# An eight-part network on one core: two VectorE programs written out without a loop, and the depthwise convolutions as 64x64 quarters

## What is computed

```python
x = x + window_attention(layernorm(x))          # layer 0: 7x7 windows, 4 heads
t = t + top2_of_8_experts(layernorm(t))         # 128x128 matrix for each expert
x = x + focal_modulation(layernorm(x))          # layer 1, below
t = t + recurrence(layernorm(t))                # 3136 steps in time, 32 in parallel

# focal modulation
y = x @ Wf + bf; q, ctx, gates = split(y)
for l, k in enumerate((k0, k1, k2)):            # depthwise 3x3, 5x5, 7x7
    ctx = gelu(depthwise_conv(ctx, k))
    ctx_all += ctx * gates[l]
ctx_all += gelu(mean_over_pixels(ctx)) * gates[3]
out = layernorm(q * (ctx_all @ Wh + bh)) * gamma + beta
out = out @ Wp + bp
```

## Time and profile before

| | |
|---|---|
| median of 3 runs | 8981.09 us (8978.25 to 9027.3) |
| the profiled execution | 8979.28 us, span 8977.5 us |
| granted TensorE clock, mean | 0.973 |
| busy | PE 90%, DVE 70%, POOL 64%, PEld 54%, ACT 50% |
| experts, about | 1.81 to 3.87 ms of the span |
| convolutions, about | 4.45 to 6.04 ms |
| focal output, about | 6.06 to 7.10 ms |

### The profile page before, as it was taken

The page is one execution under the profiler, slowest core; times in us unless marked ns, Lnnn a source line. Parts: engine busy times, 40 slices in busy tenths (PEclk is TensorE's granted clock), DMA queues, the critical chain, the costliest instruction groups (busy, mean ns, idle before and its releaser), DMA issues. The chain is left out here.

```text
span 8977.5 us, 330977 instructions
## 1 busy us (share of the span) xinstructions
PE 8051.4 (90%) x112719; PEld 4838.4 (54%) x112719; DVE 6262.3 (70%) x21127; ACT 4513.2 (50%) x12517; POOL 5701.4 (64%) x6959
## 2 busy tenths in 40 slices
PE   7999999978889898779799999988888788888888
PEld 6777777744444444357544444436666555555554
DVE  8999999979999999878656666656777622222222
ACT  5666666645555555469733333335555433333333
POOL 8999999968888888778622222225666644444444
PEclk9999999989999999989999999999999899999999
DMA  1222222211111111258844554538777422222221
GB/s 52 57 57 57 58 58 58 59 53 54 54 54 54 51 53 54 69 183 301 286 163 164 180 181 164 180 124 214 200 203 200 121 55 55 56 56 56 56 55 53
DMA packets 797656, 955.86 MB, mean 106 GB/s; under 512 B 323100, under 2 KB 661825, under 8 KB 773584
## 3 DMA queue, kind: packets, MB, share of 16 engines
q1 hardware_dynamic: 797264, 952.06, 34.7%
HBM read 574.81 MB, written 453.35 MB: 115 GB/s over the span
## 5 line engine op out<-in xcount | busy, mean ns | idle before, releaser
L982 PE MATMUL moe_pe_out<-moe_we,moe_xnT 128*128 128x512 f32 x3136 | 1530.2, 621 | 232.3 <-DVE moe_acc L876 224.9
L1587 PE MATMUL conv_pc<-conv_c,conv_toep 64*64 64x416 f32 (+1 forms) x6896 | 1335.6, 534 | 4.2 <-ACT conv_c L1488 2.7
L778 ACT ACTIVATE moe_scaled<-moe_pe_out,moe_gate 128x128 f32<-128x128 f32 x3136 | 892.5, 368 | 792.8 <-PE moe_pe_out L982 791.1
L2287 ACT ACTIVATE rec_yT<-rec_ph 128x32 f32<-128x32 f32 x3136 | 618.4, 197 | 1251.5 <-PE rec_ph L2408 1251.5
L1443 POOL TENSOR_TENSOR conv_g<-conv_c,conv_gate 128x896 f32<-128x896 f32 x128 | 365.3, 2854 | 1212.2 <-DVE conv_out L1557 1174.6
L982 PEld LDWEIGHTS moe_pe_out<-moe_we,moe_xnT 128*128 128x128 f32 x3136 | 558.5, 195 | 1032.1 <-issue 1023.8
L298 POOL TENSOR_SCALAR att_xn<-att_xin,att_mv,att_rstd 128x128 f32<-128x128 f32 x1024 | 1007.1, 997 | 54.2 <-POOL att_rstd L294 54.2
L2408 PE MATMUL rec_ph<-rec_yT,rec_vt 128*32 128x32 f32 x25080 | 853.1, 207 | 196.6 <-ACT rec_yT L2287 121.8
L2334 DVE COPY rec_xT<-rec_pin 128x512 f32<-128x512 f32 x196 | 135.6, 692 | 1250.5 <-PE rec_pin L2380 1250.5
L2408 PEld LDWEIGHTS rec_ph<-rec_yT,rec_vt 128*32 128x32 f32 x25080 | 506.5, 108 | 647.5 <-ACT rec_yT L2287 609.9
L1587 PEld LDWEIGHTS conv_pc<-conv_c,conv_toep 64*64 64x64 f32 (+1 forms) x6896 | 487.9, 144 | 604.8 <-issue 535.2
(11 more groups left out here) (210 smaller groups left out, 19573.4 us busy)
## 6 DMA issues: line engine op xcount, KB each, us to landing
conv_toep<-rows_dram SPq DMA_DIRECT2D x32, 2304.0 KB, 13.9
c<-foc_cs SPq DMA_DIRECT2D x32, 1792.0 KB, 10.9
conv_cin<-c SPq DMA_DIRECT2D x32, 1792.0 KB, 8.9
ctx_all<-conv_out SPq DMA_DIRECT2D x32, 1792.0 KB, 7.0
att_xin<-x_windows SPq DMA_DIRECT2D x512, 98.0 KB
moe_xin<-x SPq DMA_DIRECT2D x112, 448.0 KB, 3.5
x<-moe_acc SPq DMA_DIRECT2D x112, 448.0 KB, 2.7
foc_xin<-x SPq DMA_DIRECT2D x32, 1568.0 KB, 8.3
```

The lines of the kernel that those rows point to most:

```text
L778: ins = act.activation(scaled[:, b, e, :], pe_out[:, b, 1, e * C:(e + 1) * C], ACT.Identity, scale=g)
L982: pe.matmul(pe_out[:, b, half, :], xnT[:, n.slot(2), t, :], we[:, half * 4:half * 4 + 4, :].rearrange("d e c -> d (e c)"), start=True, sto ...
L1587: return pe.matmul(image_pairs(pc[k], half)[m0:m1, :, i0:i1], w, tile[r0:r1, images(half), i0 + away:i1 + away], start=start, stop=(rows ! ...
L2287: act.activation(yT[:, a, cs], ph[:, a, cs], ACT.Sigmoid).then_inc(moved, 1)
```

## The change

In the experts' and the focal output's stage VectorE's steps are written out one after the other, with constant waits, by a new helper `straight_steps`. The other engines keep their loops. In the convolutions each product is now of 64 input and 64 output partitions, 60 in a channel, and the average is four such products (`average_low`, `average_high`). The filters' halves are interleaved in a new order; three semaphores (`firsts_made`, `thirds_made`, `half_averaged`) keep the two row halves of one bank apart in time. ScalarE takes `gelu2` ahead of the average and of `gelu3_plain`.

```diff
@@ -80,6 +80,15 @@
         for u in range(unroll):
             step(Step(it, unroll, u), MANY, -MANY)
     for n in range(rounds * unroll, count):
+        step(Step(0, unroll, n), n, n - count)
+
+
+def straight_steps(count, unroll, step):
+
+
+
+
+    for n in range(count):
         step(Step(0, unroll, n), n, n - count)
 
 
@@ -947,7 +956,7 @@
                 if last < -3:
                     layer_stats_end(n + 3)
 
-            run_steps(dve, N, U, step, 4)
+            straight_steps(N, U, step)
 
         @block.tensor
         def _(pe):
@@ -1370,7 +1379,7 @@
         rows_made = S.sems("rows_made", 2)
         group_in, toep_in, c0_in = S.sems("group_in", 2), S.sems("toep_in", 2), S.sems("c0_in", 2)
         convolved = S.sems("convolved", 3)
-        corners_made = S.sem("corners_made")
+        firsts_made, thirds_made, half_averaged = S.sem("firsts_made"), S.sem("thirds_made"), S.sem("half_averaged")
         activated = S.sems("activated", 3)
         gated1, gated2, gated3 = S.sem("gated1"), S.sem("gated2"), S.sem("gated3")
         pooled_part, averaged, glob_ready = S.sem("pooled_part"), S.sem("averaged"), S.sem("glob_ready")
@@ -1503,13 +1512,12 @@
                     gelu2(n, 0)
                 if last < -3:
                     gelu1(n + 2, first + 2)
+                if last < -2:
+                    gelu2(n + 1, first + 1)
                 if first >= 1:
                     average(n - 1, first - 1)
                 if last < -1:
                     gelu3_plain(n, first)
-                if last < -2:
-                    gelu2(n + 1, first + 1)
-                if last < -1:
                     gelu3_swapped(n)
 
             run_steps(act, N + 1, U, step, AHEAD)
@@ -1585,7 +1593,7 @@
                 if k == 2 and half == 1:
                     m0, m1 = ROW - m0, ROW - m0 + ROW
                 return pe.matmul(image_pairs(pc[k], half)[m0:m1, :, i0:i1], w,
-                                 tile[r0:r1, images(half), i0 + away:i1 + away], start=start, stop=(rows != ALL), skip_group_check=True)
+                                 tile[r0:r1, images(half), i0 + away:i1 + away], start=start, stop=True, skip_group_check=True)
 
             def ready(k, n, first):
                 g = Step(n.loop, U // PER, n.off // PER)
@@ -1596,40 +1604,13 @@
                 if k > 0:
                     hold(pe, activated[k - 1], n.val(1, 1), ticks)
                 if first >= 1:
-                    pe.wait_ge(activated[k], n.val())
-
-            def centre(k, n, first):
+                    hold(pe, activated[k], n.val(), ticks)
+
+            def whole(k, n, first):
+
                 ready(k, n, first)
                 for half in range(2):
                     block_of(k, n, half, 0, start=True)
-
-            def middle_plain(n, first):
-                ready(2, n, first)
-                for away in (0, 1, -1):
-                    block_of(2, n, 0, away, start=(away == 0))
-
-            def middle_swapped(n):
-
-                for away in (0, 1, -1):
-                    for outs in (LOW, HIGH):
-                        block_of(2, n, 1, away, outs=outs, start=(away == 0))
-
-
-            def four(crossed, straight):
-
-
-
-
-                (k, n, half, far), (j, m, part, low, high) = crossed, straight
-                block_of(k, n, half, -far, HIGH, LOW)
-                block_of(j, m, part, low, LOW, HIGH if j == 2 else LOW)
-                second = block_of(j, m, part, high, HIGH, LOW if j == 2 else HIGH)
-                first = block_of(k, n, half, far, LOW, HIGH)
-                return first, second
-
-            def whole(k, n, first):
-
-                centre(k, n, first)
                 for half in range(2):
                     if k == 0:
                         block_of(0, n, half, -1, HIGH, LOW)
@@ -1639,12 +1620,68 @@
                             ins = block_of(1, n, half, away)
                 ins.then_inc(convolved[k], 1)
 
-            def average(n, first):
-                if first >= 1:
-                    pe.wait_ge(glob_ready, n.val())
-                    pe.sem_inc(ticks, 1)
-                pe.wait_ge(pooled_part, n.val(1, 1))
-                pe.matmul(pm[:, 0:B], ones[:], pooled[:], start=True, stop=True).then_inc(averaged, 1)
+            def first_filter(n, low, high, start):
+
+
+
+                block_of(0, n, high, 0, HIGH, LOW, start)
+                block_of(0, n, low, 0, LOW, LOW, start)
+                block_of(0, n, high, 0, HIGH, HIGH, start)
+                block_of(0, n, low, 0, LOW, HIGH, start)
+                block_of(0, n, high, -1, HIGH, LOW)
+                return block_of(0, n, low, 1, LOW, HIGH)
+
+            def second_filter(n, low, high, start):
+
+
+
+                block_of(1, n, low, 0, LOW, LOW, start)
+                block_of(1, n, high, 0, HIGH, HIGH, start)
+                block_of(1, n, high, 0, HIGH, LOW, start)
+                block_of(1, n, low, -1, LOW, LOW)
+                block_of(1, n, high, -1, HIGH, HIGH)
+                block_of(1, n, low, 0, LOW, HIGH, start)
+                block_of(1, n, high, -1, HIGH, LOW)
+                block_of(1, n, low, 1, LOW, LOW)
+                block_of(1, n, high, 1, HIGH, HIGH)
+                return block_of(1, n, low, 1, LOW, HIGH)
+
+            def third_filter_on_own_rows(n):
+
+
+
+                for away in (0, -1, 1):
+                    block_of(2, n, 1, away, HIGH, HIGH, away == 0)
+                    block_of(2, n, 0, away, LOW, LOW, away == 0)
+                    block_of(2, n, 1, away, HIGH, LOW, away == 0)
+                    block_of(2, n, 0, away, LOW, HIGH, away == 0)
+                block_of(2, n, 1, -2, HIGH, LOW)
+                block_of(2, n, 0, 2, LOW, HIGH).then_inc(thirds_made, 1)
+
+            def third_filter_on_other_rows(n):
+
+                block_of(2, n, 0, -2, HIGH, LOW)
+                block_of(2, n, 1, 2, LOW, HIGH)
+                for away in (0, -1, 1):
+                    block_of(2, n, 0, away, HIGH, LOW)
+                    block_of(2, n, 1, away, LOW, HIGH)
+                    block_of(2, n, 0, away, HIGH, HIGH)
+                    ins = block_of(2, n, 1, away, LOW, LOW)
+                ins.then_inc(convolved[2], 1)
+
+            def average_low(n, first):
+                if first >= 1:
+                    hold(pe, glob_ready, n.val(), ticks)
+                hold(pe, pooled_part, n.val(1, 1), ticks)
+                for m0 in (0, ROW):
+                    ins = pe.matmul(pm[m0:m0 + ROW, 0:B], ones[0:ROW, 0:ROW], pooled[0:ROW, :], start=True, stop=False)
+                ins.then_inc(half_averaged, 1)
+
+            def average_high(n):
+                hold(pe, half_averaged, n.val(1, 1), ticks)
+                for m0 in (0, ROW):
+                    ins = pe.matmul(pm[m0:m0 + ROW, 0:B], ones[ROW:P, 0:ROW], pooled[ROW:P, :], start=False, stop=True)
+                ins.then_inc(averaged, 1)
 
             def step(n, first, last):
                 has1, has2, has3 = last < -3, last < -2, last < -1
@@ -1653,37 +1690,27 @@
                     whole(0, n + 1, 1)
                     whole(1, n, 0)
                 if has1:
-                    centre(0, n + 2, first + 2)
+                    ready(0, n + 2, first + 2)
+                    first_filter(n + 2, 0, 1, True)
                 if has2:
-                    centre(1, n + 1, first + 1)
+                    ready(1, n + 1, first + 1)
+                    second_filter(n + 1, 0, 1, True).then_inc(firsts_made, 1)
+                if has3:
+                    ready(2, n, first)
+                    third_filter_on_own_rows(n)
+                if first >= 1:
+                    average_low(n - 1, first - 1)
+                if has2:
+                    hold(pe, firsts_made, n.val(1, 1), ticks)
                 if has1:
-                    four((0, n + 2, 0, 1), (1, n + 1, 0, -1, 1))
-                    made1, made2 = four((0, n + 2, 1, 1), (1, n + 1, 1, -1, 1))
-                    made1.then_inc(convolved[0], 1)
-                    made2.then_inc(corners_made, 1)
-                elif has2:
-                    for half in range(2):
-                        block_of(1, n + 1, half, -1, LOW, LOW)
-                        made2 = block_of(1, n + 1, half, 1, HIGH, HIGH)
-                    made2.then_inc(corners_made, 1)
+                    first_filter(n + 2, 1, 0, False).then_inc(convolved[0], 1)
+                if has2:
+                    second_filter(n + 1, 1, 0, False).then_inc(convolved[1], 1)
+                if first >= 1:
+                    average_high(n - 1)
                 if has3:
-                    middle_plain(n, first)
-                if first >= 1:
-                    average(n - 1, first - 1)
-                if has3:
-                    middle_swapped(n)
-                if has2:
-                    hold(pe, corners_made, n.val(2, 1), ticks)
-                    made2, _ = four((1, n + 1, 0, 1), (1, n + 1, 1, 1, -1))
```

(13 more changed lines are left out.)

## The result

The changed kernel takes 8689.54 us (median of 4 runs, 8688.08 to 8727.33), the kernel before 8979.67 beside it: a ratio of 0.9676 with a 95% interval of 0.9634 to 0.9718, 290 us less. The forecast was 8748 and the low end of its range 8695, so the direction and the mechanisms held and the gain was larger than the range allowed.

The account below looks back on a forecast made before the run. VectorE (93% busy) was full in the experts, TensorE (100%) in the convolutions, no engine in the focal output, where something interrupts all. 8979.3 - 80 - 100 - 84 + 33 = 8748 us; range 8695 to 8870.

Parts of the forecast that it names:

- Experts without a loop: Experts' stage: removing VectorE's 24 loop returns and the slower steps behind them saves 80 us.
- With 16.65 us for a written-out step: Experts' stage: 96 steps go from 17.48 to 16.65 us each, the pace of steps taken as already written out.
- Focal output without a loop: Focal output: removing VectorE's 12 loop returns takes 24 images from 31.87 to 27.7 us each, saving 100 us.
- Rival D: Focal output becomes DMA-bound and gives back 50 us: 8798 us in all; chance 0.1.
- Convolutions in quarters: Convolutions: without changes of product shape a channel takes 11.36 us instead of 12.03, 84 us less over 126.
- rival C: Convolutions: the array's quarters aren't independent, a channel takes 12.26 us, the kernel 8861 us; chance 0.2.
- about 0.27 us, and 0.07 us for joints: Convolutions: cost per channel of the average in quarters and of joints, added to 11.02 us of stream.
- The margin of 0.6 us: Convolutions: VectorE's chain takes about 10.7 us a channel, below 11.36, so TensorE stays the bound.
- Code of TensorE: Convolutions: the longer TensorE loop body stalls at its returns, 13 times 2.5 us, adding 33 us.
- Rival A: All edits pay and TensorE refetches at its returns: 8748 us, own range 8715 to 8785; chance 0.42.
- Rival B: Convolutions: no refetch at TensorE's loop returns, 8715 us in all; chance 0.23.
- Rival E: Convolutions: TensorE's instruction stream feeds the array too slowly; slower than before, 9047 us at 14 us a channel; chance 0.05.

Follow-up runs that it names:

- e11: The changed kernel with the experts' programs of TensorE, ScalarE and GpSimd written out without a loop too: 8689.21 us.
- e1: The kernel before with only VectorE's program of the experts written out: 8876.26 us, ratio 0.9896.
- e5: The kernel before with only VectorE's program of the focal output written out: 8887.72 us, one run.
- e4: The changed kernel with TensorE's program of the convolutions written out too: median 8682.57 us, four runs in two groups.
- e12: The same kernel as e4, run again with more rounds: 8656.76 us, ratio 0.9643 to the kernel before.
- e7: The changed kernel with the convolutions' average as one 128x128 product again, everything else in quarters: 8772.02 us, ratio 0.977.

## Why the prediction was right, and where it was wrong

The mechanisms of all three edits held, and the time still fell below the range, because sizes were wrong, most of them to the same side: the pace of written-out steps (16.45 us for 16.65), the average in quarters (0.10 us for 0.34), TensorE's return (2.25 us for 2.5), and the recurrence, which had no term and gave 11 us.

**Experts without a loop.** The mechanism held: 24 gaps and the slow steps behind them went, with no new gap by issue. The failed step is "With 16.65 us for a written-out step". The 96 steps went from 17.48 to 16.45 us, 99 us instead of 80. I took the seven steps of the earlier trace rows for the pace of written-out code, but only the first three of them are written out; the other four are the first pass of the loop's body, 16.47, 16.70 and 16.29 us against 16.88, 16.55, 16.96 and 16.29. In the changed kernel the same seven take 16.37. Inside the body a step is thus about 0.3 us dearer even without a return, and the three ahead of it were 0.1 dearer too. The four steps at the end, 16.71 us, were a bad guide in another way: in the changed kernel too they are slower than the mean, 16.52. e11 and e1 exclude that the other engines' loops add to it. In the trace the four steps of a body hold some 184 register instructions of VectorE that the written-out steps do not have; whether these are the 0.3 us is argued, and no run separates it.

**Focal output without a loop.** Held to 3 us: 27.78 us an image, forecast 27.7; 98 us alone in e5 and 97 together. Rival D fell: the DMA engines moved 232 GB/s at 90% over the stretch from 5980 to 6700 us and no load was late there.

**Convolutions in quarters.** Independence of the four quarters held, so rival C fell: 11.12 us a channel, where half-empty rounds would have made 12.26. The stream of 11.02 us was nearly right: from the second half of an average to the next average a stretch of 84 passes takes 7.75 us where the forecast's passes add up to 7.71. The term that was mis-sized is "about 0.27 us, and 0.07 us for joints": together they are 0.10, which makes 126 x 0.24 = 30 us more gain. I had laid the four products of the average end to end with their weight loads; in quarters they run beside the convolutions' products. The timeline shows them starting 0.04 us apart from products of 416 columns. The margin of 0.6 us that I had estimated for VectorE's chain shrank by this to 0.4 and was enough: no product waits for it.

**Code of TensorE.** Rival A has TensorE pay at 13 returns, and e4 and e12 show it: 2.25 us against 2.5, 29 us against 33. That the size came so near is luck, since I had halved a middle of VectorE's prices without a row for the half. Refetching as the reason rests on the lengths of the bodies that stall and that do not, and is not shown by itself. Rival B, no price at the returns, fell, though the time came out nearest to its number, by other errors: 8715 less the 19 and 30 us above and the recurrence's 11, plus these 29 and 3 in the focal output, is 8687. One sign was wrong: I expected a dip of TensorE's clock at each return; it stands at 1.00 over the whole stretch from 4500 to 5800 us, with all these gaps (1.9 us at most) in it. Rival E fell by far.

The Trainium skill ("Runtime: NRT & Kernel Launch", instruction fetch mechanics) gives a window of 2048 instructions for TensorE. The body of 2147 stalls, those of 1512 in attention and 1162 in the old convolutions do not, which agrees; but e7's body of 2043 stalls at each return too, so as a limit on length the figure is not safe. That run's expectation had foreseen this, because the body reaches into nine blocks of 256; no run moved it to tell length from place. For the other engines the page gives 512. There the runs differ: VectorE's 420 instructions stall at each return, in two different stages, and the measurement decides. The prediction's sentence that by that rule both VectorE loops stall was thus right of the experts' 647 instructions and, by length, not of the focal output's 420, which I had not counted. A body of 420 that the rule would let pass costs 5.0 to 8.6 us at each return.

**Recurrence.** No step covered it. I asked what each edit costs in its own stage, and not what a longer program does to the place of loops behind it. 11 us of the miss come from there.

**The range.** It ended at 8695 because I closed it 20 us below B. The mis-sized terms had been bounded on the side of loss only: the steps before 2005 us with their lowest value, 16.29, and an average that hides altogether would have made 35 + 43 us more of gain.

## What to carry to other kernels

Look for issue gaps at the first instruction of a step and count them against the loop's returns; if they match, write that engine's program out, and expect more than the gaps' sum: here 102 us for 72, and 98 for 90. When TensorE is full with products of several shapes, bring them all to one shape, down to the smallest product, and mind the length of the body that results: here writing out the stalling TensorE loop too gave another 29 us in its stage (8656.76 us in all). Take a pace from code in the very form that it will have, and keep a range as wide on the side of gain as on that of loss.

## What the hardware showed that I had not expected

- A return of a VectorE loop costs 4.9 to 6.5 us at 420 and 523 instructions in the focal input, 6.4 to 8.6 at 420 in the focal output and 2.95 to 3.2 at 647 in the experts; 283 instructions show no gap. Where between 283 and 420 the limit lies, and why, stays open. The price is lowest where the DMA engines are least busy (16% in the experts, 78% in the focal output), but no run varies their load alone. A TensorE body of 2147 costs 2.25 us and one of 2043 some 2.3; 1512 shows no gap.
- A small product of another shape between quarters costs 0.66 us more than the same product in quarters.
- The place of a TensorE loop that shows no issue gap is worth 0.1 us for each return, 10 us in the recurrence; by what rule was not tried.
- A semaphore increment costs VectorE 0.09 us.
